# Batch 1's projections placed among the first maxima, and three operands' parts made by GpSimd

## The chip, the cores and the metric

One core of a Trainium2 chip runs the whole program in one launch. It has five instruction streams that meet only through semaphores: TensorE (PE) for matrix products, VectorE (DVE), ScalarE (ACT) and GpSimd (POOL) for the rest, and SyncE (SP), which issues most of the DMAs. Each engine takes its instructions strictly in the order in which they were written. The time is the device time of one execution in microseconds; the kernel before took 1213.18 us (median of 3 runs, 1212.56 to 1214.47).

## The reference

Four batches of 1024 tokens with 128 features go through three steps, each on the layer-normalised input and added to it: an expert-choice feed-forward (8 experts, each takes the 256 tokens of a batch with the highest affinity), attention with 16 heads of 8 features and rotary angles in three axes, and the same feed-forward again.

```python
x = x + 0.5 * ffn(layernorm(x))
x = x + attn(layernorm(x))
x = x + 0.5 * ffn(layernorm(x))

# ffn: affinity = softmax(x @ gate.T); per expert the 256 best tokens of a batch
h = silu(x_in @ w_gate.T) * (x_in @ w_up.T)
out[tokens of the expert] += gating * (h @ w_down.T)

# attn
q, k, v = x @ Wq + bq, x @ Wk + bk, x @ Wv + bv      # 16 heads of 8
q, k = rope3d(q), rope3d(k)                          # y * cos + rotated(y) * sin
out = softmax(q @ k.T / sqrt(8)) @ v @ Wo + bo
```

## The kernel before

**Passes.** The feed-forward runs as 16 passes (it = 0 to 15) before attention and 16 behind it; a pass is one expert on two batches. Batches 0 and 1 are done in passes 0 to 7, batches 2 and 3 in 8 to 15. A pass has four gate and up products (`gate_up`), the down product of the pass before (`down`), its outputs, and the choice and gathering of tokens for later passes. Its three weights come in two buffers each, loaded by `load_weights(j)` on SyncE; `gate_up(j, 0)` waits for all three. GpSimd issues the gathers of rows and the scatters that add the outputs to x in DRAM.

**Side work.** Between the products of a pass stand small steps at places (it, k), set by the table `place` in `tables()`. The keys ("s", m) are the preparation of attention for batches 0 and 1: m = 0 the rotated weights, 1 to 4 the transposes of the normalised x into ZT, and from 5 on five steps for each operand u. An operand u is q or k of batch u // 2 (u = 0 is q of batch 0, u = 3 is k of batch 1). Its five steps are four projections (w in two halves of 512 tokens, then the rotated weights wr in two halves) and one of values. In these steps VectorE adds the bias and multiplies by cos or sin (L1677), and adds the two products (L1692).

**Parts.** q and k are used in bfloat16 as sums of three parts, so each operand of 128 x 1024 goes through `high` (ScalarE rounds it, L934), `rest` (the operand less that part), `middle` (ScalarE rounds the rest, L938) and `lowest` (the rest less the middle part). For u = 0 and 1 VectorE does rest and lowest, for the others GpSimd (L673, L678). The parts stand in two buffers (u % 2) and go to DRAM (`store_parts`), from where `load(q)` fetches the rows of a group of heads. SyncE does all this in the order in which it is written, the weights among it.

**First maxima.** Attention has 16 groups, q = 0 to 15, four to a batch, so batch 1 is used from group 4 on. A group first needs the maximum of each row of scores: 32 pieces of two matmuls into one of two pA buffers (L1373), and a VectorE reduction for each (L1821). Behind pass 15 the 32 pieces of group 0 and 12 of group 1 run by themselves. Among them stands what is left of the preparation, in a table `window`: "T" are transposes for batches 2 and 3, "PR" the four projections of operands 4 to 7, into the three pS banks in rotation, with a value step into pO behind the fourth, and "m" the turn of the first maxima. Here ScalarE adds the bias (L1059), and GpSimd multiplies (`product`, L683) and adds (`add_products`, L688). VectorE computes the moments of batches 2 and 3 behind pieces 12 and 13 and their `scale_and_shift` behind 14 and 15; ScalarE takes the roots (`deviation`) and normalises (`normalise(6)`, `normalise(7)`).

**Groups.** Then group q runs its 64 score matmuls (L1458), 64 exponentials on ScalarE (L1115), 64 products with the values (L1437), and among them the pieces of the next groups. Behind 46 exponentials TensorE turns the next group's maxima (L1381), which GpSimd has cut in parts (`maxima`, L693 to L699), and ScalarE copies them as mT (L1124). In groups 0 and 1 ScalarE also has `middle(5)`, `high(6)`, `high(7)`, `middle(6)` and `middle(7)` between its exponentials.

Of the kernel before, what the change touches and what calls it, by code (L numbers as in the profile page):

```python
# [12 lines left out]
B, N, D = 4, 1024, 128  # L13
# [3 lines left out]
P = 128  # L17
CH = N // P
T = B * CH
# [10 lines left out]
NF = 11 + ROUNDS  # L30
# [13 lines left out]
def tables():  # L44
# [6 lines left out]
    for m in range(5, 25):  # L51
        place[divmod(55 + m, 5)] = ("s", m)
# [32 lines left out]
    for u, at in ((4, 22), (5, 28), (6, 32), (7, 37)):  # L85
        for i in range(4):
            window[divmod(at + i, 32)] = ("PR", u, i)
# [4 lines left out]
def program(nc, t, x1, out, zd, qk, vp, md, ud, dd, rd):  # L92
    ctx = ExitStack()
    with ctx:
# [6 lines left out]
        def sem(name):  # L101
# [114 lines left out]
        pairs = {4: (scr[:, 0, :], scr[:, 2, :]), 5: (scr[:, 1, :], scr[:, 3, :]), 6: (room[:, 0, :], room[:, 1, :]),  # L216
                 7: (U[1][:, :], U[2][:, :])}
# [161 lines left out]
        def _(sp):  # L379
# [55 lines left out]
            def store_values(b):  # L435
                if b < 2:
                    sp.wait_ge(*was_read(("s", 10 * b + 14)))
                else:
                    sp.wait_ge(s_vs, 2 * b - 2)
# [104 lines left out]
            store_values(1)  # L544
            load_weights(16)
            load_weights(17)
            for b in range(2, B):
                sp.wait_ge(s_scat[b], 256)
                load_x(b, x1_in)
            store_parts(2)  # L550
# [51 lines left out]
        def _(pool):  # L602
# [76 lines left out]

            def product(u, i):  # L680
# [4 lines left out]
            def add_products(u):  # L685
                a, b = pairs[u]
                pool.wait_ge(s_mul, 2 * (u - 3))
# [117 lines left out]
            scatter(RUN - 1)  # L805
            rest(2)
            rest(3)
            lowest(2)
# [21 lines left out]
            product(7, 1)  # L830
            lowest(5)
            add_products(7)
            rest(6)
# [7 lines left out]
            for q in range(1, NQ):  # L841
                if q in (7, 11, 15):
                    context(q // 4 - 1)
                maxima(q)
                if q == 1:
                    lowest(6)
                    rest(7)
                    lowest(7)
# [38 lines left out]
        def _(act):  # L887
# [152 lines left out]
            middle(2)  # L1040
            middle(3)

# [19 lines left out]
            def value_rows(u):  # L1062
                act.wait_ge(s_v, u - 3)
                values_out(u, pO[:, :]).then_inc(s_vs, 1)

            deviation(6)
            deviation(7)
            act.wait_ge(s_sd, 8)
            S.activation(warm[:, :], sd[:, 0:8], ACT.Exp)
            normalise(6)  # L1070
            turned_half(0)
            turned_half(1)
            normalise(7)
# [28 lines left out]
            def result(q, half):  # L1102
                k = q % 3
                act.wait_ge(s_pv, 16 * q + 8 * half + 12)
                act.wait_ge(s_ust[k], 128 * (q // 3) + 16)
                S.activation(U[k][:, half * 512:(half + 1) * 512], pO[:, :], ACT.Copy).then_inc(s_U, 1)  # L1106

            def group(q):
                k = q % 3
                for s in range(16):  # L1110
# [840 lines left out]
```

## Time and profile before

| | us |
|---|---|
| median of 3 runs | 1213.18 |
| profiled execution, its own time | 1224.46 |
| its span, first to last instruction | 1222.7 |
| TensorE busy in it | 1085.8 (89%) |
| VectorE busy | 981.3 (80%) |
| ScalarE busy | 774.1 (63%) |
| GpSimd busy | 580.7 (47%) |

The profile is one execution, recorded by the hardware. Passes 0 to 15 take the first 308 us of it, the first maxima 308 to 372, the 16 groups 372 to about 960, and the second feed-forward the rest. A row of a timeline gives start, length, engine, line, operation, result and source, how many were merged, and in brackets how long the engine had been idle before and what ended that. A number such as L1373 is a line of the kernel. The lengths of neighbours overlap by some tenths of a microsecond, since a record ends when the last result is written. "PEclk", the clock column, is the granted share of 2.4 GHz: 1.00, or 0.50 for 1.2 GHz.

### The profile page before, as it was taken

What the parts mean: (1) busy time and instruction counts of PE and PEld (TensorE: products, weight loads), DVE (VectorE), ACT (ScalarE), POOL (GpSimd) and SP (SyncE); (2) the same over time, 40 slices, a digit from 0 to 9 for tenths busy, and PEclk for the clock granted to TensorE, in tenths of its full rate; (3) what the DMA queues carried; (4) which work ended last, traced back from release to release, by engine and by line L of the source; (5) the groups of instructions that cost most, each with busy time, mean ns of one, the idle gap of its engine ahead of it and who ended that gap; (6) DMA issues with size and microseconds to landing.
All of it is one profiled execution on the core that took longest, in us unless ns stands there. A gap on an engine that the chain in (4) does not pass through costs nothing. (4 is left out here: it accounts for less than half of the span.)

```text
span 1222.7 us, 25195 instructions
## 1 busy us (share of the span) xinstructions
PE 1085.8 (89%) x9412; PEld 471.6 (39%) x9412; DVE 981.3 (80%) x1938; ACT 774.1 (63%) x1466; POOL 580.7 (47%) x610
## 2 busy tenths in 40 slices
PE   6189899899499899999999999999999889899994
PEld 6056566566132122222222222222222247566663
DVE  5755966565979899999999999999997576876641
ACT  3044232532258899999989999899999936222220
POOL 4035878665456331000011476355621077677886
PEclk6589999999688899999999999999999999999997
DMA  9014456448703131211021111211220126345553
GB/s 268 27 44 115 89 100 142 93 79 185 192 36 96 33 90 43 58 43 47 21 58 42 42 51 40 53 42 41 64 68 11 24 66 151 82 90 102 113 101 29
DMA packets 93072, 93.84 MB, mean 77 GB/s; under 512 B 14684, under 2 KB 70236, under 8 KB 92920
## 3 DMA queue, kind: packets, MB, share of 16 engines
q1 hardware_dynamic: 70424, 75.46, 22.2%
q0 software_dynamic: 22528, 16.79, 10.4%
q8 instruction: 74, 1.21, 0.4%
q14 instruction: 46, 0.38, 0.1%
HBM read 64.02 MB, written 30.13 MB: 77 GB/s over the span
## 5 line engine op out<-in xcount | busy, mean ns | idle before, releaser
L1821 DVE TENSOR_REDUCE mx<-pA 128x2 f32<-128x1024 f32 x512 | 585.9, 1217 | 20.1 <-PE pA L1373 19.4
L1115 ACT ACTIVATE Pt<-pS 128x512 f32<-128x512 f32 x1024 | 556.3, 596 | 34.5 <-PE pS L1458 29.0
L1437 PE MATMUL pO<-Pt,Vst 128*16 128x256 f32 x4096 | 322.7, 387 | 13.4 <-ACT U L1106 12.8
L1012 ACT ACTIVATE Pt<-pS 128x512 f32<-128x512 f32 x128 | 76.3, 596 | 206.9 <-PE pS L1287 177.4
L622 POOL DMA_INDIRECT xg<-zd,idx x128 | 125.9, 983 | 165.0 <-DVE idx L1628 95.1
L1373 PE MATMUL pA<-Kst,Qst 48*128 48x512 bf16 x704 | 140.8, 397 | 20.1 <-DVE mx L1821 18.4
L1287 PE MATMUL pS<-Pt,wg 128*128 128x512 f32 x256 | 139.8, 629 | 13.4 <-issue 7.5
L1437 PEld LDWEIGHTS pO<-Pt,Vst 128*16 128x16 f32 x4096 | 68.2, 94 | 207.0 <-issue 109.1
L1458 PE MATMUL pS<-Qst,Kst 51*128 51x512 bf16 x704 | 139.2, 391 | 7.5 <-ACT Pt L1115 4.6
L693 POOL TENSOR_TENSOR mparts<-mx,onesm 128x32 bf16<-128x32 f32 x16 | 4.0, 252 | 262.4 <-DVE mx L1826 206.2
L1298 PEld LDWEIGHTS pA<-wd,Pt 128*128 128x128 f32 x960 | 113.5, 192 | 17.0 <-issue 17.0
L1613 DVE TENSOR_SCALAR onehot<-slots,slotT 128x256 bf16<-128x256 bf16 x512 | 119.1, 312 | 0.4
L645 POOL DMA_INDIRECT x<-Pt,idx x64 | 102.3, 1598 | 32.0 <-issue 17.4
L1298 PE MATMUL pA<-wd,Pt 128*128 128x128 f32 x960 | 114.2, 275 | 0.0
L1458 PEld LDWEIGHTS pS<-Qst,Kst 51*128 51x128 bf16 x704 | 34.4, 92 | 157.3 <-ACT Pt L1115 144.3
L1655 DVE TENSOR_TENSOR Pt<-Pt,pS 128x512 f32<-128x512 f32 x64 | 43.9, 686 | 37.0 <-PE pS L1288 16.8
L1288 PE MATMUL pS<-Pt,wu 128*128 128x512 f32 x128 | 68.7, 619 | 0.0
L1288 PE MATMUL pO<-Pt,wu 128*128 128x512 f32 x128 | 66.3, 600 | 0.0
L1655 DVE TENSOR_TENSOR Pt<-Pt,pO 128x512 f32<-128x512 f32 x64 | 43.8, 685 | 27.3 <-PE pO L1288 18.8
L1458 PE MATMUL pS<-pair 51*128 51x512 bf16 x320 | 62.4, 386 | 1.1 <-ACT Pt L1115 0.4
L1373 PE MATMUL pA<-pair 48*128 48x512 bf16 x320 | 61.9, 383 | 0.6 <-DVE mx L1821 0.6
L1003 ACT ACTIVATE Pt<-pA 128x512 f32<-128x512 f32 x32 | 19.1, 597 | 67.5 <-remote 48.6
(224 smaller groups left out, 1181.7 us busy)
## 6 DMA issues: line engine op xcount, KB each, us to landing
wg<-w_gate_dram SPq DMA_DIRECT2D x32, 256.0 KB
wu<-w_up_dram SPq DMA_DIRECT2D x32, 256.0 KB
wd<-w_down_dram SPq DMA_DIRECT2D x32, 256.0 KB
qk<-parts SPq DMA_DIRECT2D x64, 96.0 KB
Kst<-qk SPq DMA_DIRECT2D x132, 32.0 KB
zd<-Z SPq DMA_DIRECT2D x8, 512.0 KB
vp<-pair SPq DMA_DIRECT2D x4, 1024.0 KB, 4.6
Vst<-vp SPq DMA_DIRECT2D x16, 256.0 KB
```

Source lines behind the costliest of these rows:

```text
L622: pool.indirect_dma_start(xg[p][:, k, :], None, zd[j // E % 2], bass.IndirectOffsetOnAxis(idx[j % 6][:, k:k + 1], 0)).then_inc(s_gath[p], 16)
L645: pool.indirect_dma_start(acc, bass.IndirectOffsetOnAxis(rows[j % 6][:, k:k + 1], 0), ye[j % 2][:, k, :], None, compute_op=ALU.add).then_i ...
L1115: S.activation(Pt[:, s % 4, j, r * 512:(r + 1) * 512], pS[:, bank_of(k, 4 * s + 2 * j + r), :], ACT.Exp, scale=SCALE).then_inc(s_exp, 1)
L1287: M.matmul(pG[u % 2], wg[p][:, u * P:(u + 1) * P], xt[:, p, :], start=True, stop=True).then_inc(s_gate, 1)
L1288: M.matmul(pU[u % 2], wu[p][:, u * P:(u + 1) * P], xt[:, p, :], start=True, stop=True).then_inc(s_up, 1)
L1298: last = M.matmul(pY[:, k * D:(k + 1) * D], hid[p][:, i, k * P:(k + 1) * P], wd[p][:, i, :], start=(i == 0), stop=(i == IC - 1))
L1373: last = M.matmul(pA[ring[q, a] % 2][:, r, :], Qst[k][64 * r:64 * r + 48, j, c * P:(c + 1) * P], Kst[k][64 * r:64 * r + 48, j, half * 512: ...
L1437: last = M.matmul(pO[32 * h:32 * h + 16, cols], Vst[k][:, s % 8, h, :], Pt[:, s % 4, h // 2, (h % 2) * 512 + 256 * a:(h % 2) * 512 + 256 * ...
L1458: last = M.matmul(pS[:, bank_of(k, n + r), :], Kst[k][64 * r:64 * r + ROWS, j, (s % 8) * P:(s % 8 + 1) * P], Qst[k][64 * r:64 * r + ROWS, ...
L1613: last = V.tensor_scalar(onehot[:, b, c, :], slots[:, :], slotT[j // E % 2][:, c * HB + b, e:e + 1], None, ALU.is_equal)
L1655: V.tensor_tensor(hid[it % 2][:, u, :], sg[:, u % 2, :], pU[u % 2], ALU.mult).then_inc(s_hid, 1)
L1821: V.reduce_max(mx2[:, k, 2 * j:2 * j + 2, c, half], pA[ring[q, a] % 2][:, :, :], AX.X).then_inc(s_Ar, 1)
```

## The change

Operands 2 and 3 (batch 1) leave passes 14 and 15 and become "PR" entries of the window, at pieces 0, 2, 4, 6 and 8, 10, 12, 13. With that ScalarE adds their bias and GpSimd multiplies and adds, where VectorE did both. The steps `high(2)`, `middle(2)`, `high(3)` and `middle(3)` of ScalarE move in between its work for the normalisations, and the value store of batch 1 moves behind the loads of x on SyncE. The high and middle parts of operands 6 and 7 and the middle part of 5 are made by GpSimd with a product with ones (`own_part`), and GpSimd's second maxima stand ahead of operand 7's sum instead of behind it. The last down product no longer waits for step ("s", 24).

```diff
-    for m in range(5, 25):
+    for m in range(5, 15):
         place[divmod(55 + m, 5)] = ("s", m)
...
-    for u, at in ((4, 22), (5, 28), (6, 32), (7, 37)):
-        for i in range(4):
-            window[divmod(at + i, 32)] = ("PR", u, i)
+    for u, ats in ((2, (0, 2, 4, 6)), (3, (8, 10, 12, 13)), (4, range(22, 26)), (5, range(28, 32)), (6, range(32, 36)), (7, range(37, 41))):
+        for i, at in enumerate(ats):
+            window[divmod(at, 32)] = ("PR", u, i)
...
             load(0)
             load(1)
-            store_values(1)
             load_weights(16)
             load_weights(17)
             for b in range(2, B):
                 sp.wait_ge(s_scat[b], 256)
                 load_x(b, x1_in)
+            store_values(1)
             store_parts(2)
...
+            def own_part(u, i, ready):
+                a = pairs[u][i]
+                pool.wait_ge(*ready)
+                if i == 0:
+                    pool.wait_ge(s_partst[u % 2], 128 * (u // 2))
+                GP.tensor_tensor(parts[:, u % 2, i, :].rearrange("p (a n) -> p a n", n=P), a.rearrange("p (a n) -> p a n", n=P),
+                                 ones[:, :].unsqueeze(1).to_broadcast([P, N // P, P]), ALU.mult).then_inc((s_hi, s_mid)[i], 1)
...
             scatter(RUN - 1)
+            product(2, 0)
+            product(2, 1)
+            add_products(2)
+            product(3, 0)
             rest(2)
+            product(3, 1)
+            add_products(3)
+            lowest(2)
             rest(3)
-            lowest(2)
             lowest(3)
...
             product(7, 1)
+            own_part(5, 1, (s_rest, 6))
             lowest(5)
+            own_part(6, 0, (s_roped, 7))
+            rest(6)
+            maxima(1)
+            own_part(6, 1, (s_rest, 7))
+            lowest(6)
             add_products(7)
-            rest(6)
+            own_part(7, 0, (s_roped, 8))
+            rest(7)
+            own_part(7, 1, (s_rest, 8))
+            lowest(7)
...
-                maxima(q)
-                if q == 1:
-                    lowest(6)
-                    rest(7)
-                    lowest(7)
+                if q > 1:
+                    maxima(q)
...
-            middle(2)
-            middle(3)
...
+            for u in (2, 3):
+                for i in range(4):
+                    projected(u, i)
+                value_rows(u)
+            high(2)
             deviation(6)
+            middle(2)
             deviation(7)
             act.wait_ge(s_sd, 8)
             S.activation(warm[:, :], sd[:, 0:8], ACT.Exp)
             normalise(6)
+            high(3)
             turned_half(0)
             turned_half(1)
+            middle(3)
             normalise(7)
...
-                    if q == 0 and s == 8:
-                        middle(5)
-                    if q == 0 and s == 9:
-                        high(6)
-                    if q == 0 and s == 13:
-                        high(7)
-                    if q == 0 and s == 15:
-                        middle(6)
-                    if q == 1 and s == 2:
-                        middle(7)
...
-                pe.wait_ge(*was_read(("s", 24) if j < RUN else ("f", 3, NF - 1)))
+                pe.wait_ge(*was_read(("s", 14) if j < RUN else ("f", 3, NF - 1)))
```

TensorE, pass 15 and the start of the first maxima. L1287 and L1288 are gate and up, L1298 and L1313 down, L1206 a projection, L1212 a value step, L1373 a piece. Before:

```order
L1206 MATMUL pA<-ZT,wq 128x512
L1298 MATMUL pA<-wd,Pt 128x128 x8
L1206 MATMUL pA<-ZT,wr 128x512
L1287 MATMUL pS<-Pt,wg 128x512
L1288 MATMUL pS<-Pt,wu 128x512
L1206 MATMUL pA<-ZT,wr 128x512
L1287 MATMUL pS<-Pt,wg 128x512
L1288 MATMUL pO<-Pt,wu 128x512
L1212 MATMUL pA<-wv,ZT 128x128 x4
L1313 MATMUL pA<-wd,Pt 128x128 x16
L1373 MATMUL pA<-Kst,Qst 128x512 x42
```

and now (L1306, L1307, L1317, L1332, L1225, L1231 and L1392 are the same functions):

```order
L1317 MATMUL pA<-wd,Pt 128x128 x16
L1306 MATMUL pS<-Pt,wg 128x512
L1307 MATMUL pS<-Pt,wu 128x512
L1306 MATMUL pS<-Pt,wg 128x512
L1307 MATMUL pO<-Pt,wu 128x512
L1332 MATMUL pA<-wd,Pt 128x128 x16
L1392 MATMUL pA<-Kst,Qst 128x512 x2
L1225 MATMUL pS<-ZT,wq 128x512
L1392 MATMUL pA<-Kst,Qst 128x512 x4
L1225 MATMUL pS<-ZT,wq 128x512
L1392 MATMUL pA<-Kst,Qst 128x512 x4
L1225 MATMUL pS<-ZT,wr 128x512
```

The five steps have left the pass, and projections stand between the pieces from the first on.

GpSimd, from the last scatters (L645) to the product of operand 4. Before:

```order
L645 DMA x<-Pt,idx 2048x128 x16
L673 TENSOR_TENSOR scr<-scr,parts 128x1024 x2
L678 TENSOR_TENSOR parts<-scr,parts 128x1024 x2
L683 TENSOR_TENSOR scr<-scr,cos 128x1024
L683 TENSOR_TENSOR scr<-scr,sin 128x1024
L688 TENSOR_TENSOR scr<-scr 128x1024
```

and now (L693 is `product`, L698 `add_products`, L674 `rest`, L679 `lowest`):

```order
L646 DMA x<-Pt,idx 2048x128 x16
L693 TENSOR_TENSOR scr<-scr,cos 128x1024
L693 TENSOR_TENSOR scr<-scr,sin 128x1024
L698 TENSOR_TENSOR scr<-scr 128x1024
L693 TENSOR_TENSOR scr<-scr,cos 128x1024
L674 TENSOR_TENSOR scr<-scr,parts 128x1024
L693 TENSOR_TENSOR scr<-scr,sin 128x1024
L698 TENSOR_TENSOR scr<-scr 128x1024
L679 TENSOR_TENSOR parts<-scr,parts 128x1024
L674 TENSOR_TENSOR scr<-scr,parts 128x1024
L679 TENSOR_TENSOR parts<-scr,parts 128x1024
L693 TENSOR_TENSOR scr<-scr,cos 128x1024
```

Six operations have come in ahead of operand 4, and the parts of 2 and 3 are made between them.

GpSimd in groups 0 and 1, from the last products of operand 7 (U) on, with the second maxima (mparts). Before:

```order
L683 TENSOR_TENSOR U<-U,sin 128x1024
L678 TENSOR_TENSOR parts<-scr,parts 128x1024
L688 TENSOR_TENSOR U<-U 128x1024
L673 TENSOR_TENSOR onehot<-onehot,parts 128x1024
L693 TENSOR_TENSOR mparts<-mx,onesm 128x4x8
L695 TENSOR_TENSOR mres<-mx,mparts 128x32
L697 TENSOR_TENSOR mparts<-mres,onesm 128x4x8
L699 TENSOR_TENSOR mparts<-mres,mparts 128x4x8
L678 TENSOR_TENSOR parts<-onehot,parts 128x1024
L673 TENSOR_TENSOR U<-U,parts 128x1024
L678 TENSOR_TENSOR parts<-U,parts 128x1024
```

and now (L687 is `own_part`):

```order
L693 TENSOR_TENSOR U<-U,sin 128x1024
L687 TENSOR_TENSOR parts<-scr,ones 128x1024
L679 TENSOR_TENSOR parts<-scr,parts 128x1024
L687 TENSOR_TENSOR parts<-onehot,ones 128x1024
L674 TENSOR_TENSOR onehot<-onehot,parts 128x1024
L703 TENSOR_TENSOR mparts<-mx,onesm 128x4x8
L705 TENSOR_TENSOR mres<-mx,mparts 128x32
L707 TENSOR_TENSOR mparts<-mres,onesm 128x4x8
L709 TENSOR_TENSOR mparts<-mres,mparts 128x4x8
L687 TENSOR_TENSOR parts<-onehot,ones 128x1024
L679 TENSOR_TENSOR parts<-onehot,parts 128x1024
L698 TENSOR_TENSOR U<-U 128x1024
```

Products with ones have come in, two of them ahead of the maxima (five in all, the last two behind the sum of operand 7), and that sum stands behind the maxima.

## Rows read from the trace of the kernel before

**Rows 1.** Busy time by stage; columns: stretch, its length, busy of each engine, clock, DMA
```profile
272.40:287.60 15.20, 15.20 (x70) 9.41 (x69) 9.91 (x16) 5.66 (x11) 11.02 (x7) 1.00 0.92 220
...
308.50:336.00 27.50, 11.11 (x40) 2.01 (x40) 26.82 (x58) 8.38 (x15) 14.11 (x8) 0.56 0.73 177
...
372.40:411.00 38.60, 33.32 (x275) 6.76 (x273) 33.02 (x28) 30.26 (x55) 22.26 (x14) 0.78 0.38 97
...
447.40:484.00 36.60, 35.68 (x389) 8.56 (x385) 36.54 (x34) 35.62 (x69) 4.19 (x13) 1.00 0.17 36
```

**Rows 2.** Timeline of TensorE around passes 14 and 15; start, us, instruction, idle before
```profile
278.49 1.02 PE L1206 MATMUL pA<-ZT,wq 128*128 128x512 f32 x2
...
286.72 1.05 PE L1212 MATMUL pA<-wv,ZT 128*128 128x128 f32 x8
...
303.62 3.81 PE L1313 MATMUL pA<-wd,Pt 128*128 128x128 f32 x32 [1.08 <-ACT pair L926]
308.54 0.61 PE L1373 MATMUL pA<-Kst,Qst 48*128 48x512 bf16 x4 [1.11 <-DVE Pt L1646]
```

**Rows 3.** Timeline of SyncE's DMA issues behind pass 13
```profile
273.84 6.69 SPq L432 DMA_DIRECT2D qk<-parts  x8
...
281.62 0.49 SPq L395 DMA_DIRECT2D wd<-w_down_dram  x1
...
297.47 0.35 SPq L463 DMA_DIRECT2D Vst<-vp  x1
```

**Rows 4.** Busy time in two stretches of pass 14; last columns: DMA share, GB/s
```profile
273.40:277.10 3.70, 3.70 (x13) 1.79 (x12) 2.25 (x3) 2.01 (x3) 3.09 (x3) 1.00 0.84 292
...
281.00:285.50 4.50, 4.50 (x17) 2.30 (x16) 3.81 (x8) 1.19 (x2) 2.28 (x1) 1.00 1.05 255
```

**Rows 5.** Timeline of TensorE, a projection at either clock
```profile
342.57 2.08 PE L1206 MATMUL pS<-ZT,wq 128*128 128x512 f32 x2
...
352.42 1.13 PE L1206 MATMUL pS<-ZT,wq 128*128 128x512 f32 x2
```

**Rows 6.** Timeline of VectorE, first maxima and group 0
```profile
308.97 14.80 DVE L1821 TENSOR_REDUCE mx<-pA 128x2 f32<-128x1024 f32 x13 [0.94 <-PE pA L1373]
...
331.03 0.17 DVE L1528 SCALAR_TENSOR_TENSOR shift<-mv,rstd 128x8 f32<-128x8 f32 x1
...
399.40 2.12 DVE L1826 TENSOR_TENSOR mx<-mx 128x32 f32<-128x32 f32 x1
...
444.49 0.19 DVE L1826 TENSOR_TENSOR mx<-mx 128x32 f32<-128x32 f32 x1
```

**Rows 7.** Timeline of GpSimd, from the last scatter to group 0
```profile
314.75 1.56 POOL L645 DMA_INDIRECT x<-Pt,idx  x1 [0.30 <-issue]
...
345.45 2.34 POOL L683 TENSOR_TENSOR scr<-scr,cos 128x1024 f32<-128x1024 f32 x1 [20.77 <-ACT scr L1059]
...
381.57 2.35 POOL L683 TENSOR_TENSOR U<-U,cos 128x1024 f32<-128x1024 f32 x1
...
399.12 2.36 POOL L688 TENSOR_TENSOR U<-U 128x1024 f32<-128x1024 f32 x1
```

**Rows 8.** Timeline of ScalarE, groups 0 to 2
```profile
373.08 1.10 ACT L1115 ACTIVATE Pt<-pS 128x512 f32<-128x512 f32 x2
...
383.98 12.03 ACT L1115 ACTIVATE Pt<-pS 128x512 f32<-128x512 f32 x22 [0.68 <-PE pS L1458]
395.89 1.06 ACT L938 ACTIVATE parts<-scr 128x1024 bf16<-128x1024 f32 x1
...
405.24 0.27 ACT L1124 ACTIVATE mT<-pS 96x128 bf16<-96x128 bf16 x1 [1.64 <-PE pS L1381]
...
447.35 0.28 ACT L1124 ACTIVATE mT<-pS 96x128 bf16<-96x128 bf16 x1
...
483.98 0.27 ACT L1124 ACTIVATE mT<-pS 96x128 bf16<-96x128 bf16 x1
```

**Rows 9.** Timeline of TensorE, group 0
```profile
404.89 0.31 PE L1381 MATMUL pS<-identb,mparts 128*96 128x128 bf16 x1 [2.42 <-POOL mparts L699]
```

More of the change, by code:

```diff
@@ L215, in program @@
         room = onehot[:, :, :, :].rearrange("p b c s -> p (b c s)").bitcast(F32).rearrange("p (i n) -> p i n", i=2)
-        pairs = {4: (scr[:, 0, :], scr[:, 2, :]), 5: (scr[:, 1, :], scr[:, 3, :]), 6: (room[:, 0, :], room[:, 1, :]),
-                 7: (U[1][:, :], U[2][:, :])}
+        pairs = {u: (scr[:, u % 2, :], scr[:, 2 + u % 2, :]) for u in range(2, 6)}
+        pairs |= {6: (room[:, 0, :], room[:, 1, :]),
+                  7: (U[1][:, :], U[2][:, :])}
         dens = sb("dens", [P, P], F32)
@@ L435, in store_values @@
             def store_values(b):
-                if b < 2:
-                    sp.wait_ge(*was_read(("s", 10 * b + 14)))
+                if b == 0:
+                    sp.wait_ge(*was_read(("s", 14)))
                 else:
-                    sp.wait_ge(s_vs, 2 * b - 2)
+                    sp.wait_ge(s_vs, 2 * b)
                 sp.dma_start(vp[b * G:(b + 1) * G].rearrange("g p f -> p g f"),
@@ L686, in add_products @@
                 a, b = pairs[u]
-                pool.wait_ge(s_mul, 2 * (u - 3))
+                pool.wait_ge(s_mul, 2 * (u - 1))
                 GP.tensor_tensor(a, a, b, ALU.add).then_inc(s_roped, 1)
@@ L1062, in value_rows @@
             def value_rows(u):
-                act.wait_ge(s_v, u - 3)
+                act.wait_ge(s_v, u - 1)
                 values_out(u, pO[:, :]).then_inc(s_vs, 1)
+            for u in (2, 3):
[3 more added lines that the diff above has]
+            high(2)
             deviation(6)
+            middle(2)
             deviation(7)
@@ L1105, in result @@
                 act.wait_ge(s_ust[k], 128 * (q // 3) + 16)
+                if (q, half) == (1, 0):
+                    act.wait_ge(s_parts, 2 * B)
                 S.activation(U[k][:, half * 512:(half + 1) * 512], pO[:, :], ACT.Copy).then_inc(s_U, 1)
@@ L1397, in window_use @@
                     if i == 0:
-                        pe.wait_ge(s_winr, win["T", 2 * (b - 2) + 1] + 1)
-                    last = project(op, (wq, wr)[i // 2], 2 * (b - 2) + i % 2, bank)
+                        pe.wait_ge(*(was_read(("s", 4)) if b == 1 else (s_winr, win["T", 2 * (b - 2) + 1] + 1)))
+                    last = project(op, (wq, wr)[i // 2], 2 * (b % 2) + i % 2, bank)
                 else:
@@ L1405, in window_use @@
                     u = key[1]
-                    if u > 4:
-                        pe.wait_ge(s_vs, u - 4)
+                    if u > 2:
+                        pe.wait_ge(s_vs, u - 2)
                     project_values(u, pO[:, :]).then_inc(s_v, 1)
@@ L1414, in _ @@
             pe.wait_ge(s_ye, RUN)
-            pe.wait_ge(*was_read(("s", 24)))
+            pe.wait_ge(*was_read(("s", 14)))
             pe.nop().then_inc(s_mt, 1)
@@ L1425, in _ @@
             pe.wait_ge(s_winr, len(win))
-            pe.wait_ge(s_vs, 4)
+            pe.wait_ge(s_vs, 6)
             pe.nop().then_inc(s_pv, 4)
```

## Prediction

> **What bounds the kernel now.** I read the busy time by stage first [rows 1]. In passes 14 and 15 TensorE is full (15.20 us of 15.20). In the first maxima (308.5 to 336.0) VectorE is full (26.82 of 27.5) and TensorE idles at half its clock. In the first two attention groups (372.4 to 411.0) nobody is full and the mean clock is 0.78; from 447.4 on VectorE is at 36.54 of 36.60. So the three stages that the change touches have three limits, and each of its parts is priced in its own. What is won there carries to the end: the groups behind run at a fixed pace (next paragraph), and nothing they load is late.
>
> The pace of a group is read from ScalarE's copy mT, once a group [rows 8]: 447.35 to 483.98 is 36.63 us, the steady value. 405.24 to 447.35 is 42.11, so 5.5 us are lost there. From the group's first exponential (373.08) to 405.24 are 32.2 us, where a steady group takes 46 exponentials at 0.545 (22 of them in 12.03), one result copy before and one after (1.1): 26.2. Lost: 6.0. Together 11.5 us.
>
> Durations are of the profiled execution: span 1222.7, its own time 1224.5, 11 us above the median 1213.18 that I predict from; I take the difference over unscaled (scaling by 0.99 changes it by 0.1).
>
> **Passes 14 and 15 (term A).** Each loses 4 projections and 4 value matmuls on TensorE. A projection shows 1.02 us [rows 2], two back to back start 0.86 apart as the records overlap, a value step 0.89 from 1.05: 4 x 0.86 + 0.89 = 4.33 us a pass, all on the path, since TensorE is full. In pass 15 also the 1.08 us go in which the last down product waited for ScalarE's value copy [rows 2]. If TensorE stays the limit: 2 x 4.33 + 1.08 = 9.7 us.
>
> What is late next in pass 14 is its successor's weights. SyncE issues pass 15's weights behind eight part stores (273.84, 6.69 us) and ends at 281.62 + 0.49 = 282.1 [rows 3]. Nothing in that chain moves: it hangs on batch 0's values, which stay in pass 13. The DMA engines are full, share 1.05 from 281.0 to 285.5. Up to 277.1 they move 292 GB/s x 3.7 us = 1.08 MB, which is the value store [rows 4]. Behind it come 0.77 MB of parts, 0.77 of weights and a scatter (0.3 with what it reads), 1.85 MB at pass 14's 220 GB/s [rows 1]: 8.4 us, weights in at 285.5. TensorE would want them at 287.61 - 4.33 = 283.3; today it comes at 287.6 and never notices. So pass 14 gives 1.9, not 4.3 (ends: 0 if they land at 287.6, 4.3 if at 283.3). Waiting 2.4 us may also drop the clock: TensorE's 2.42 us wait at 404.9 was followed by 5.5 us at 1.2 GHz [rows 9]. Half a chance of 1 us: 0.5.
>
> Then the first maxima's operands. store_parts(1) comes 2 us earlier, its landing at most 1 (full DMA engines), so load(0), whose last issue is 297.47 [rows 3], ends near 297 and lands near 299.5. TensorE arrives at 285.5 + (308.54 - 287.61) - 4.33 - 1.08 = 301.0: no new wait. Term A: -1.9 - 5.4 + 0.5 = -6.8; ends -9.0 (held by load(0)) and -3.9.
>
> **First maxima, 44 pieces (term B).** S is the first piece (308.54 now). VectorE takes 13 pieces in 14.80 us, 1.13 each [rows 6]. Added: 8 projections and 2 value steps on TensorE among pieces 0 to 13. At 2.4 GHz a projection is 1.13 with 1.06 between starts, at 1.2 GHz 2.08 and 2.0 [rows 5]; a piece takes 0.33 or 0.6 on TensorE. Fast: 14 x 0.33 + 8 x 1.06 + 2 x 0.95 = 15.0 against VectorE's 15.8: hidden, save 0.5 where a value step bunches. Slow throughout: 28.2, of which some 5 lie beside batch 2's moments on VectorE: +7.6. Today the clock falls 3.4 us into this stage because TensorE idles, which it would no longer do; I take the fast end, +0.7.
>
> On GpSimd six operations of 2.35 come in (14.1 us) before batch 2's first product, today at 345.45 after 20.77 us idle [rows 7]: 6.7 us of room, part of which goes in waits for high and middle, and ScalarE's two high and two middle copies stand between its normalisations. I follow the chain: the last scatter ends at S + 7.8 as now (it hangs on the last outputs), products and sum of operand 2 at S + 15, first product of 3 at 17.3, high(2) 18.3, rest 20.5, sum of 3 at 25.2, high(3) 26.2 to 27.4, rest(3) 29.6, lowest(3) 34.5. Batch 2's product starts at S + 36.9 now. Fits by 2.4. high(3) stands ahead of the ZT copies at S + 29.3: fits. middle(3) delays normalise(7) by 1.0, of which 0.5 arrives.
>
> VectorE itself is touched. Its 128x32 maximum takes 0.19 us in the other groups, but 2.12 at 399.40, exactly while GpSimd's sum runs from 399.12 for 2.36 [rows 6, 7]: a two-operand VectorE instruction waits for a GpSimd instruction that reads. Today GpSimd is idle from 324.7 to 345.4, over all of batch 2's and 3's moments; now it computes there. Exposed are veps twice and shift twice (0.17 each [rows 6]), each against a 2.1 to 2.35 us operation: nothing to 9.4 us, a mean of 1.2 where GpSimd is busy. By the times above veps(6) falls in a gap, the other three hit for 1.8, 0.8 and 0.7: +3.0. Pieces before 20 set the end, so this is on the path; it hides the 0.5 of middle(3). The Trainium skill has this rule ("SBUF — State Buffer", Who interferes with whom): a VectorE instruction with two SBUF inputs, or in a two-port mode, and a reading GpSimd instruction block each other whole, while a reduction never takes part. The reductions agree: 1.13 each, though GpSimd computes beside the last seven of the 13. Without the rule term B would be 3 us smaller.
>
> Term B: +0.7 + 3.0 = +3.7; ends 0 and +12. SyncE: store_values(1) only moves behind two X loads; batch 1 is first loaded at group 2.
>
> **First two groups (term C).** The 11.5 lost consist of: five ScalarE copies of 0.95 (395.89 is one [rows 8]), 4.75; a 1.2 GHz stretch at the start, 14 exponentials from 373.08 to 383.98 instead of in 7.6, 3.3; the wait of TensorE for GpSimd's maxima (2.42 [rows 9]) and the slow stretch behind it, the rest, 3.5. The five copies go to GpSimd at about 2.35. Maxima 1 stand seven operations behind 381.57 [rows 7]: 15.7, at 397.3, with VectorE's maximum not before 399: no wait, and no collision as GpSimd waits then. The other part stores follow by 416, needed at group 4. The 3.3 stay, since nothing before them on TensorE changes, and the pace cannot beat VectorE's 36.63: 0.4 more. Term C: -(11.5 - 3.3 - 0.4) = -7.8; ends -3.5 (only the wait goes) and -11.
>
> **Sum.** -6.8 + 3.7 - 7.8 = -10.9. I forecast 1202.5 us.
>
> **Rivals.**
> R1, weights bind pass 15 fully and the added projections meet the slow clock: -3.9 + 7.5 + 3.0 - 7.8 is about -1 at the extreme; the middle of it -5: 1208. For: the full DMA engines, the half clock in this stage. Against: TensorE would be busy there.
> R2, GpSimd's port costs nothing and the clock stays up: -9.0 + 0.7 - 7.8 = -16: 1197. Against: the 2.12 row.
> R3, the copies moved off ScalarE buy little because VectorE, next at 36.54 of 36.60, is the limit, and the slow stretch spreads: term C -3.5, total -6.6: 1206.5. Against: VectorE idles whenever those copies run (33.0 of 38.6).
> R4, slower: the in-order chain GpSimd-ScalarE for batch 1. high(3) stands ahead of the ZT copies and needs GpSimd's eighth step. The chain has 3 us of room at high(3); each us by which the first product comes later than S + 12 delays group 0 by one. At S + 27 it eats the 14.6 of A and C; at S + 30 the time is 3 slower, 1216. It needs the last scatters to land 20 us late; they end at 316.3 now [rows 7], though into full DMA engines.
> R5, no net effect: B near +11, within 0.2% (2.4 us, about what a measurement of this kernel can tell from no change).
>
> **Chances.** Forecast (1199 to 1206) 0.55, R2 0.12, R1 0.13, R3 0.10, R4 0.04, R5 0.06. Range 1196 to 1209. Faster by over 0.2% 0.90, within 0.06, slower 0.04.
>
> **What would show it.** A: gate_up of pass 15 starts near 285.5 after an idle, first piece near 301.5; wrong if the idle is missing (then -9) or the piece is after 304.5. B: 1.1 us projections between pieces, first group 66 to 68 us after the first piece (63.9 now), VectorE's small instructions of 1 to 2.4 us; wrong if they stay at 0.17. C: mT at 36.7 instead of 42.1 between groups 0 and 1, no TensorE wait on GpSimd there. The forecast is wrong if batch 1's parts are what batch 2's ZT copies wait for.

## The result and the profile after

The changed kernel took 1207.53 us (median of 5 runs, 1204.31 to 1210.77), the kernel before 1213.52 beside it: ratio 0.9946, 95% interval 0.9929 to 0.9964, that is 6.5 us less (4.4 to 8.6). The recorded ratio isn't the quotient of the medians; these are 6.0 apart. A second session gave 1207.03 against 1213.60, ratio 0.9945 (0.9927 to 0.9963). I had forecast 10.9 less. The sign and the three parts are right; the terms A and B have a wrong size, and 1207.53 lies outside the band of 1199 to 1206 that I gave my own account, though inside the whole range. Two executions far longer than all others, 1512.09 us of the kernel before and 2499.92 of before_gate, are left out of all ratios.

Spans can't be subtracted here. Pass 14 starts at 272.41 in the trace before and at 265.15 in the one after, though nothing ahead of it differs; over all profiled executions of this study it starts anywhere from 260.3 to 274.2. From there to the end the two take 950.3 and 943.8, which are 6.5 apart as the times are. So every trace below is read from pass 14's start, in three stretches that answer to the three terms: to the first piece (A), from there to the first exponential of group 0 (B), and from there to the second copy mT that follows, 447.35 in [rows 8] (C).

| us | A | B | C | A+B+C |
|---|---|---|---|---|
| before | 36.13 | 64.54 | 74.27 | 174.94 |
| after | 32.51 | 71.13 | 64.50 | 168.14 |
| difference | -3.6 | +6.6 | -9.8 | -6.8 |
| forecast | -6.8 | +3.7 | -7.8 | -10.9 |
| after, second session | 32.87 | 67.92 | 64.35 | 165.14 |

The busy time by stage of the changed kernel, columns as in [rows 1]:

```profile
265.10:279.30 14.20, 11.09 (x54) 6.86 (x53) 6.21 (x11) 5.66 (x11) 10.61 (x8) 0.97 0.90 231
279.30:297.70 18.40, 17.25 (x82) 11.42 (x82) 5.00 (x12) 2.39 (x4) 7.71 (x6) 0.84 0.68 151
297.70:325.00 27.30, 16.43 (x66) 6.00 (x66) 26.09 (x52) 12.33 (x24) 23.33 (x13) 0.90 0.57 156
368.80:406.70 37.90, 36.61 (x351) 8.27 (x351) 36.90 (x35) 34.88 (x67) 35.85 (x20) 0.91 0.37 92
433.30:469.90 36.60, 35.67 (x389) 8.57 (x385) 36.54 (x34) 35.64 (x68) 4.27 (x13) 1.00 0.14 36
```

Pass 14 is no longer full (11.09 us of 14.20). The first maxima now run at a clock of 0.90 instead of 0.56, with VectorE still the full engine and GpSimd at 23.33 instead of 14.11. The groups behind are what they were.

**A.** The first matmuls of passes 14 and 15 in the kernel before:

```profile
272.41 1.02 PE L1287 MATMUL pS<-Pt,wg 128*128 128x512 f32 x2
...
287.61 1.02 PE L1287 MATMUL pS<-Pt,wg 128*128 128x512 f32 x2
```

The changed kernel at the same places and up to the first piece:

```profile
265.15 1.02 PE L1306 MATMUL pS<-Pt,wg 128*128 128x512 f32 x2
...
275.17 1.02 PE L1307 MATMUL pO<-Pt,wu 128*128 128x512 f32 x2
279.34 2.05 PE L1306 MATMUL pS<-Pt,wg 128*128 128x512 f32 x2 [3.15 <-issue]
281.18 1.91 PE L1307 MATMUL pS<-Pt,wu 128*128 128x512 f32 x2
282.88 1.91 PE L1306 MATMUL pS<-Pt,wg 128*128 128x512 f32 x2
284.59 1.39 PE L1307 MATMUL pO<-Pt,wu 128*128 128x512 f32 x2
285.81 3.73 PE L1317 MATMUL pA<-wd,Pt 128*128 128x128 f32 x32
...
297.66 0.39 PE L1392 MATMUL pA<-Kst,Qst 48*128 48x512 bf16 x2 [1.11 <-DVE Pt L1665]
```

Pass 15 starts 14.19 us after pass 14 instead of 15.20, behind an idle of 3.15 us. This row names nothing that ended the idle; that it was the weights is shown below, by issuing them earlier. And its four gate and up steps, 3.44 us at 2.4 GHz (4 x 0.86), take 6.47 (279.34 to 285.81): they run at 1.2 GHz, all but the end of the last.

SyncE over the same time, for [rows 3]:

```profile
266.58 7.13 SPq L433 DMA_DIRECT2D qk<-parts  x8
...
274.76 0.46 SPq L396 DMA_DIRECT2D wd<-w_down_dram  x1
275.27 5.05 SPq L433 DMA_DIRECT2D qk<-parts  x8
282.86 2.14 SPq L462 DMA_DIRECT2D Qst<-qk  x6
```

**B.** VectorE's small instructions, 0.17 us each before [rows 6]. veps is the variance plus epsilon, shift the mean times the reciprocal of the deviation, each for batch 2 and then for batch 3:

```profile
315.99 2.10 DVE L1542 TENSOR_SCALAR veps<-mv 128x8 f32<-128x8 f32 x1
...
321.48 1.00 DVE L1542 TENSOR_SCALAR veps<-mv 128x8 f32<-128x8 f32 x1
...
323.74 1.14 DVE L1547 SCALAR_TENSOR_TENSOR shift<-mv,rstd 128x8 f32<-128x8 f32 x1
...
326.16 0.80 DVE L1547 SCALAR_TENSOR_TENSOR shift<-mv,rstd 128x8 f32<-128x8 f32 x1
```

Together 5.04 instead of 0.68. GpSimd beside them now runs one instruction right behind the other, where it was idle for 20.77 us before [rows 7]:

```profile
315.72 2.34 POOL L693 TENSOR_TENSOR scr<-scr,cos 128x1024 f32<-128x1024 f32 x1
318.02 2.12 POOL L674 TENSOR_TENSOR scr<-scr,parts 128x1024 f32<-128x1024 f32 x1
...
339.82 2.35 POOL L693 TENSOR_TENSOR scr<-scr,cos 128x1024 f32<-128x1024 f32 x1 [2.39 <-ACT scr L1078]
```

The first veps starts 0.27 us behind a product of 2.34 and ends with it. The last row is batch 2's first product: GpSimd still waits 2.39 us for ScalarE before it, so R4's chain is not what sets the end. Batch 2's first projection on TensorE is the mark by which B is split further down:

```profile
334.43 2.04 PE L1225 MATMUL pS<-ZT,wq 128*128 128x512 f32 x2 [0.23 <-ACT ZT L1068]
```

**C.** ScalarE in the first groups, for [rows 8], and GpSimd's second maxima:

```profile
368.79 2.19 ACT L1144 ACTIVATE Pt<-pS 128x512 f32<-128x512 f32 x4
...
377.64 15.32 ACT L1144 ACTIVATE Pt<-pS 128x512 f32<-128x512 f32 x28 [0.87 <-PE pS L1477]
...
396.65 0.27 ACT L1153 ACTIVATE mT<-pS 96x128 bf16<-96x128 bf16 x1
...
433.29 0.27 ACT L1153 ACTIVATE mT<-pS 96x128 bf16<-96x128 bf16 x1
```
```profile
394.10 0.25 POOL L703 TENSOR_TENSOR mparts<-mx,onesm 128x32 bf16<-128x32 f32 x1 [0.96 <-DVE mx L1845]
```

28 exponentials run in a row where one of the part copies came after 22, and the two copies mT are 36.64 us apart, the steady pace, where they were 42.11. It is GpSimd that waits for VectorE now (0.96 us), not TensorE for GpSimd (2.42 [rows 9]).

### The profile page after: what moved, and what is told of

It reads as the page before. It is cut to its first block and busy times, and to the rows that moved or that the text cites. A ratio compares the mean times of both kernels' runs of the same rounds, so it can differ in the third digit from the quotient of the medians.

```text
span 1208.9 us, 25202 instructions
## 1 busy us (share of the span) xinstructions
PE 1084.2 (90%) x9412; PEld 474.2 (39%) x9412; DVE 976.4 (81%) x1928; ACT 775.5 (64%) x1469; POOL 606.4 (50%) x621
## 3 DMA queue, kind: packets, MB, share of 16 engines
q8 instruction: 74, 1.21, 0.4%
## 5 line engine op out<-in xcount | busy, mean ns | idle before, releaser
L1392 PE MATMUL pA<-Kst,Qst 48*128 48x512 bf16 x704 | 137.8, 388 | 18.5 <-DVE mx L1840 17.4
L1306 PE MATMUL pS<-Pt,wg 128*128 128x512 f32 x256 | 140.7, 632 | 7.7 <-issue 4.9
L1317 PEld LDWEIGHTS pA<-wd,Pt 128*128 128x128 f32 x960 | 114.0, 193 | 16.9 <-issue 16.1
L1317 PE MATMUL pA<-wd,Pt 128*128 128x128 f32 x960 | 114.5, 276 | 0.0
L1307 PE MATMUL pS<-Pt,wu 128*128 128x512 f32 x128 | 68.4, 617 | 0.0
L1307 PE MATMUL pO<-Pt,wu 128*128 128x512 f32 x128 | 67.5, 610 | 0.0
L1392 PE MATMUL pA<-pair 48*128 48x512 bf16 x320 | 61.2, 378 | 0.6 <-DVE mx L1840 0.6
```

Of the source, the lines that this page charges most:

```text
L1306: M.matmul(pG[u % 2], wg[p][:, u * P:(u + 1) * P], xt[:, p, :], start=True, stop=True).then_inc(s_gate, 1)
L1307: M.matmul(pU[u % 2], wu[p][:, u * P:(u + 1) * P], xt[:, p, :], start=True, stop=True).then_inc(s_up, 1)
L1317: last = M.matmul(pY[:, k * D:(k + 1) * D], hid[p][:, i, k * P:(k + 1) * P], wd[p][:, i, :], start=(i == 0), stop=(i == IC - 1))
L1392: last = M.matmul(pA[ring[q, a] % 2][:, r, :], Qst[k][64 * r:64 * r + 48, j, c * P:(c + 1) * P], Kst[k][64 * r:64 * r + 48, j, half * 512: ...
```

## The experiments

Eleven kernels (one of them the changed kernel again), in three sessions: the first four of the table behind "before", the next four, and the last three. Each was timed beside the kernel before, whose median was 1222.68, 1213.60 and 1226.12 in them, so only ratios carry over. The table gives the ratio with its interval, what it makes of the session's time before, and the stretches of the one profiled execution. Single executions differ by some us outside the three stretches too; the stretches show the mechanism, the ratio the size, and where the two disagree the text says so.

| kernel | ratio (95%) | us | A | B | C | sum |
|---|---|---|---|---|---|---|
| before | | | 36.13 | 64.54 | 74.27 | 174.94 |
| parts_only | 0.9941 (0.9919-0.9964) | -7.2 | 36.16 | 64.77 | 65.56 | 166.49 |
| proj_only | 0.9973 (0.9950-0.9995) | -3.3 | 32.03 | 68.86 | 74.27 | 175.16 |
| weights_first | 0.9943 (0.9922-0.9963) | -7.0 | 29.65 | 69.23 | 64.80 | 163.68 |
| kept_warm | 0.9964 (0.9950-0.9979) | -4.4 | 32.44 | 69.05 | 65.52 | 167.01 |
| after_again | 0.9945 (0.9927-0.9963) | -6.7 | 32.87 | 67.92 | 64.35 | 165.14 |
| gate_first | 0.9888 (0.9864-0.9912) | -13.6 | 27.87 | 69.15 | 65.59 | 162.61 |
| kept_warm_short | 0.9919 (0.9893-0.9946) | -9.8 | 29.95 | 68.14 | 64.91 | 163.00 |
| reductions | 0.9931 (0.9909-0.9952) | -8.4 | 31.66 | 65.47 | 65.48 | 162.61 |
| before_gate | 1.0000 (0.9987-1.0013) | 0.0 | 36.13 | 63.39 | 73.29 | 172.81 |
| gate_eps | 0.9894 (0.9874-0.9914) | -13.0 | 28.36 | 67.01 | 65.02 | 160.39 |
| warm_turn | 0.9857 (0.9822-0.9892) | -17.5 | 27.14 | 63.27 | 65.65 | 156.06 |

**The parts alone.**
```
 kernel before, and in GpSimd's program:
+            own_part(5, 1, (s_rest, 6))
             lowest(5)
+            own_part(6, 0, (s_roped, 7)); rest(6); maxima(1); own_part(6, 1, (s_rest, 7)); lowest(6)
             add_products(7)
+            own_part(7, 0, (s_roped, 8)); rest(7); own_part(7, 1, (s_rest, 8)); lowest(7)
-                    (ScalarE's middle(5), high(6), high(7), middle(6), middle(7) in groups 0 and 1)
```


> The kernel before with the parts' half of the change alone (operand 5's second part and operands 6 and 7's parts made by GpSimd, second maxima ahead of them); batch 1's projections stay in passes 14 and 15. Theory 1 (the stages add up, as the changed kernel's trace has them: first exponential to second copy mT 64.5 us where the kernel before has 74.3): 9.8 us less than before, 1203.7 us; nothing else in the trace moves. The prediction's term C, -7.8, would be 1205.7. Rival R3 (VectorE is the limit once ScalarE is relieved, only TensorE's wait for the second maxima goes): -3.5, 1210. If the gain needs the later start of the changed kernel's attention (parts stores that would otherwise collide), it is also under 5.

7.2 us less (4.4 to 9.9; the medians are 6.3 apart); A and B as before to 0.3 us, C 65.56 instead of 74.27, 8.7 less. R3's 3.5 lies outside the interval of the ratio. The gain doesn't need the other half.

**Batch 1's projections alone.**
```
 changed kernel, and in GpSimd's and ScalarE's programs the lines above back as in the kernel before
```


> The changed kernel with the parts' half undone: only batch 1's projections are moved among the first maxima. Theory 1 (stages add): the changed kernel's trace has -3.6 in passes 14 and 15 and +6.6 from the first piece to the first exponential, so this kernel is 3.0 us slower than the kernel before, 1216.5. The prediction's terms A and B, -6.8 and +3.7, would make it 3.1 faster, 1210.4. Rival: the move pays only together with the other half or not at all, within 1 us of before. In the trace: first piece 32.5 us after pass 14's start as in the changed kernel, first exponential 71 us behind it.

C is 74.27 to the digit, A is 4.1 less and B 4.3 more: in the trace the move gives nothing (+0.2). Its 12 runs lie between 1213.33 and 1224.66, four of them up to 1217.53 and eight from 1220.36 on, and the profiled one is the slowest. The ratio says 3.3 less (0.6 to 6.1), the medians are only 0.7 apart. So the +3.0 that I had read out of the first trace after was too dark, and the forecast's -3.1 is inside the interval, but between nothing and 6 us the experiment doesn't decide. The ratios of the two halves add up to -10.5 where the changed kernel has -6.5 and -6.7, which their intervals allow; the stretches add up to -8.2 against -6.8 and -9.8.

**All of pass 15's weights ahead of batch 0's value store**, gate and up ahead of its part stores too.
```
-            store_values(0)
+            sp.wait_ge(s_up, 56);    wg, wu of pass 15
             store_parts(0)
-            load_weights(15)
+            sp.wait_ge(s_down, 14);  wd of pass 15
+            store_values(0)
             store_parts(1)
```


> The changed kernel with pass 15's three weight transfers issued ahead of batch 0's part stores and value store (wg and wu after their buffers are free, wd next). Theory 1 (TensorE's 3.15 us idle before pass 15's first gate and up product is the landing of the weights, and the 1.2 GHz stretch behind it, 279.34 to 285.81 instead of 3.44 us, is the price of that idle): both go, first piece 26.5 to 28 us after pass 14's start instead of 32.5, up to 6 us faster than the changed kernel, unless the first maxima's X operand or the batch-0 parts now land late: then 2 to 4. Rival (idle ends by something else, the weights have landed): 0, same idle. Second rival (the full DMA engines only pass the delay on): the idle is gone but TensorE waits the same time before the first piece, 0.

As the lines above show, only gate and up stand ahead of the part stores; the down weights stand behind the first eight of them.

The idle and the half clock behind it are gone, pass 15 starts 10.88 us after pass 14 and its four steps take 3.44: the idle was the wait for the weights. But the first piece gains only 2.9 of 6.3 us, as it now waits itself:

```profile
300.35 0.53 PE L1396 MATMUL pA<-Kst,Qst 48*128 48x512 bf16 x2 [4.60 <-DMA Vst<-vp]
300.81 2.07 PE L1229 MATMUL pS<-ZT,wq 128*128 128x512 f32 x2
```

The operand load behind batch 0's stores is the next wait, and the clock falls in front of the first projection. The time (-7.0) doesn't differ from the changed kernel's (-6.5 and -6.7 in the other sessions).

**TensorE kept busy through the wait, too long and right.**
```
 at the end of pass 14:
+                    pe.wait_ge(s_ye, 14)
+                    for n in range(28):      # kept_warm_short: 12
+                        M.matmul(pY[:, 0:P], ones[:, :], ones[:, :], start=True, stop=True)
```


> The changed kernel with 28 matmuls of 128x128 on constants, into a bank that is rewritten, put on TensorE at the end of pass 14, where it otherwise waits 3.15 us for pass 15's weights. They are extra work and no part of the result. Theory 1 (the half clock behind the wait costs 3.0 us of its own): the idle is filled, the clock stays at 2.4 GHz into pass 15, 2.5 to 3.0 us faster than the changed kernel though it does more work. Rival (the slow gate and up products wait for weights that arrive in pieces, or the clock falls for another reason): 0, or up to 0.5 slower for the added work.

> The changed kernel with 12 instead of 28 matmuls on constants at the end of pass 14. 28 took 6.42 us, past the landing of the weights, so that run lost 2.9 us and gained the 3.0 of the half clock: nothing in the sum. 12 take 2.75, within the 3.15 us wait. Theory 1 (the half clock is the price of TensorE's wait): pass 15 starts 14.2 us after pass 14 and runs at full clock, first piece 29.5 us after pass 14's start, 3.0 faster than the changed kernel. Rival (the clock needs more than this little work): the stretch at 1.2 GHz stays, 0.

With 28 the added work lasts 6.42 us and pass 15 starts 2.9 us later than in the changed kernel, yet the first piece comes at 32.44 (32.51 there): the half clock is gone and pays for it. The 2.5 to 3.0 us that I expected to gain didn't come, since the added work outlasts the wait. With 12, TensorE's timeline reads:

```profile
274.04 2.84 PE L1361 MATMUL pA<-ones 128*128 128x128 f32 x24
277.71 1.10 PE L1306 MATMUL pS<-Pt,wg 128*128 128x512 f32 x2 [0.83 <-issue]
278.64 1.02 PE L1307 MATMUL pS<-Pt,wu 128*128 128x512 f32 x2
```

The weights land no sooner (14.56 us after pass 14's start, 14.83 in the changed kernel beside it), but the steps behind run at full clock: first piece at 29.95 instead of 32.87, and 9.8 us under the kernel before where the changed kernel is 6.7. Behind pass 15's start the changed kernel takes 18.04 us beside it and 18.32 in its first run, this one 15.39: the half clock is worth 2.6 to 2.9 us in the trace, which is shown by adding work. In time the gain over the changed kernel is likely, but the two intervals overlap.

**The changed kernel again**, as the yardstick of that session.

> The changed kernel itself, unaltered, as the yardstick for the others on the same chip. Its first profiled execution had 103.6 us from pass 14's start to the first exponential, the three kernels with batch 1 moved that were run since had 98.9 to 101.5. If 71.1 us from the first piece to the first exponential was partly luck (VectorE's small instructions met GpSimd for 4.4 us, and the clock rose 1.3 us later than elsewhere), this run has 69 to 70; if it belongs to the kernel, 71 again. Time against the kernel before: -4 to -9 us by the first runs.

B is 67.92, and the whole difference to 71.13 lies behind batch 2's first projection (36.82 us behind the first piece here, 36.77 there): here the clock rises 2 us after it, there 9 us. So 1.6 either way of B is no property of the kernel. veps and shift took 5.07 us together here too.

**Gate and up weights first, value store ahead of the down weights.**
```
-            store_values(0)
+            sp.wait_ge(s_up, 56);    wg, wu of pass 15
             store_parts(0)
-            load_weights(15)
+            store_values(0)
+            sp.wait_ge(s_down, 14);  wd of pass 15
             store_parts(1)
```


> The changed kernel with pass 15's gate and up weights ahead of batch 0's part stores, then the parts, the value store, and the down weights last. In the run with all three weights first the 3.15 us idle and the half clock behind it were gone, but TensorE waited 4.60 us before the first piece, for an operand load that starts once batch 0's parts and values have landed (19.0 us after pass 14's start against 17.7 in the changed kernel); its value store was issued at 7.6 us. Theory 1: with the value store at about 5 us the load starts near 17.7 again, TensorE waits 3 us there, first piece 28.3 us after pass 14's start (32.5 in the changed kernel, 29.65 with all three first): 4.2 faster than the changed kernel. Rival (the DMA engines are full, bytes decide and not their order): 29.6, the wait only stays where it was. Second rival (the down weights come too late now): an idle appears before pass 15's first down product.

```profile
272.66 1.10 PE L1310 MATMUL pS<-Pt,wg 128*128 128x512 f32 x2 [1.34 <-issue]
...
288.15 0.39 PE L1396 MATMUL pA<-Kst,Qst 48*128 48x512 bf16 x2 [1.24 <-DMA Vst<-vp]
```

Two waits of 1.3 us in place of one of 3.15 and one of 4.60, neither followed by a slow stretch, and none before the down product. First piece at 27.87 (expected 28.3), and the time is 13.6 us under the kernel before: 6.9 better than the changed kernel in the same session, with intervals apart. It was the order of the issues, not the bytes.

The traces of that session show only part of the 6.9. A is 5.0 shorter than in the changed kernel, B and C are 1.2 longer each, and from pass 14's start to the end the two take 937.5 and 940.4. The other 4.4 us of the profiled pair lie ahead of pass 14, where the kernels are the same: between 200 and 240 us the mean clock is 1.00 in this execution and 0.91 to 0.92 in the other. Whether that goes with the kernel or with the execution no run decides. So the 5.0 of A are shown to be the order's, the rest of the 6.9 is not.

**The same order in the kernel before.**
```
 kernel before, with the five lines of gate_first
```


> The kernel before with one edit: pass 15's gate and up weights issued ahead of batch 0's part stores, the value store behind those, the down weights last. The same order made the changed kernel 7.0 us faster by the medians (-6.6 against -13.6 to the kernel before). Theory 1 (that gain is only the wait which the change opened): here TensorE has its four projections and a value step in either pass and the weights land before it asks for them, so nothing moves, within 1 us of the kernel before; pass 14 to pass 15 15.2 us, first piece 36.1 behind pass 14's start. Rival (the old order costs the kernel before too, through full DMA engines): 2 to 5 us faster.

Ratio 1.0000 within 0.13%; A is 36.13 as before. The order is worth something only once the projections are gone from pass 14: what it repairs is the wait that the change opened.

**Reductions in place of the four small instructions.** This kernel leaves out epsilon and the product with the reciprocal, so it measures the four instructions and can't replace them.
```
+                if i in (6, 7):
+                    V.reduce_max(veps[:, tiles(i)], mv[:, tiles(i), 1:2], AX.X).then_inc(s_ve, 1)
+                    return
 (shift likewise from mv[:, tiles(i), 0:1])
```


> The changed kernel with veps and shift of batches 2 and 3 computed by VectorE reductions of one input: epsilon and the product with the deviation's reciprocal are left out of them. Theory 1 (a VectorE instruction of that kind waits for a GpSimd instruction that reads, a reduction does not): all four take 0.2 us instead of 2.10, 1.00, 1.14 and 0.80, and the first exponential comes 3.4 to 4.4 us earlier after the first piece than in the changed kernel, near 66 to 66.7 (64.5 in the kernel before). Rival (they are slow because of what they are or where they stand, not because of GpSimd, or the first maxima are bound elsewhere): durations as before or the time given back before ZT, 0 to 1.

```profile
313.37 0.16 DVE L1543 TENSOR_REDUCE veps<-mv 128x8 f32<-128x8 f32 x1
...
316.92 0.16 DVE L1543 TENSOR_REDUCE veps<-mv 128x8 f32<-128x8 f32 x1
...
318.36 0.16 DVE L1551 TENSOR_REDUCE shift<-mv 128x8 f32<-128x8 f32 x1
...
319.79 0.16 DVE L1551 TENSOR_REDUCE shift<-mv 128x8 f32<-128x8 f32 x1
```
```profile
327.42 2.05 PE L1225 MATMUL pS<-ZT,wq 128*128 128x512 f32 x2 [0.24 <-ACT ZT L1068]
```

Same place, same size, GpSimd computing beside them: 0.16 each. Batch 2's first projection comes 32.38 us after the first piece instead of 36.77, so the 4.4 us were on the path to that mark, to the last tenth. By the medians 1.7 of it reaches the end, but the intervals overlap. The Trainium skill ("SBUF — State Buffer", Who interferes with whom) has exactly this split, reductions free and an instruction with two SBUF inputs or in a two-port mode locked out; the runs agree, 0.16 against 0.80 to 2.10.

**Epsilon by ScalarE, and TensorE kept busy in the first maxima.** Two versions on top of gate_first, with the full result.
```
 gate_eps:
+                    S.activation(sd[:, tiles(i)], mv[:, tiles(i), 1], ACT.Sqrt, bias=eps[:, :]).then_inc(s_sd, 1)
                     (for i in (6, 7), and VectorE's veps instruction is gone for them)
 warm_turn, behind pieces 14 to 19 besides:
+            DUMMIES = {14: 5, 15: 10, 16: 6, 17: 4, 18: 3, 19: 3}
+                    pe.wait_ge(s_vs, 2)
+                    for n in range(DUMMIES[a]):
+                        M.matmul(pO[:, 0:P], ones[:, :], ones[:, :], start=True, stop=True)
```


> The changed kernel with pass 15's gate and up weights first, and epsilon of batches 2 and 3 added by ScalarE as the bias of its square root instead of by a VectorE instruction. That instruction took 0.41 and 1.74 us in the run with the gate weights first (2.10 and 1.00 in the changed kernel) where it takes 0.17 beside an idle GpSimd. Port theory: 1.8 us fewer from the first piece to the first projection of batch 2 (35.83 there), 34.0; but the two shifts, earlier now, may meet GpSimd's next operation for longer than 1.15 and 0.80: then 34 to 35.8. Rival (the rest of the chain decides): 35.8 again. The epsilon by bias adds nothing on ScalarE.

> The kernel with gate weights first and epsilon as a bias, and 31 matmuls of 128x128 on constants behind pieces 14 to 19, where TensorE otherwise waits for VectorE's moments and shifts (4.74, 1.82 and 1.47 us idle). Extra work, no part of the result. Theory (the half clock under batch 2's first four projections, 2.07 us each instead of 1.13, is the price of those waits, and sits on the path): full clock there, four projections and their pieces in 5.5 instead of 8.1 us, so 2.5 to 3.3 us fewer from batch 2's first projection to the first exponential, and 3 us off the time. Rival: the added matmuls delay pieces as much as they save, 0 or slower; or the clock falls all the same and they cost 1 to 3 us.

gate_eps has batch 2's first projection at 34.58 us behind the first piece instead of 35.83 in gate_first. It waited 2.08 us before its first piece, and one of the projections behind took 2.07 us, so its moments began 16.81 us behind the first piece instead of 15.98; from there on the gain is 2.1. But its ratio is gate_first's: inconclusive in time. In warm_turn the projections that took 2.07 take 1.10 to 1.13:

```profile
332.69 1.10 PE L1234 MATMUL pS<-ZT,wq 128*128 128x512 f32 x2 [0.23 <-ACT ZT L1077]
...
334.04 1.13 PE L1234 MATMUL pS<-ZT,wq 128*128 128x512 f32 x2
```

B is 63.27, below the kernel before, although 31 matmuls were added: 3.7 less than in gate_eps (67.01), of which 1.8 behind batch 2's first projection (30.62 instead of 32.43) and 1.9 ahead of it, where pieces too ran at half clock. Of the 1.9, 0.8 is gate_eps's slow projection, ahead of the added matmuls (15.98 us to the moments here), so they are worth 2.9 in this pair of executions, within the 2.5 to 3.3 expected. 17.5 us under the kernel before (13 to 22; the medians are 16.7 apart) is the best kernel of the study. That it beats gate_eps itself (-13.0) is likely, but their intervals overlap.

## Why the prediction was right, and where its sizes were wrong

**The mechanism of A was right, its price was not.** The idle before pass 15 was forecast at 2.4 us and is 3.15, so pass 14 gives 1.0 and not 1.9. The step that failed is the clock: "Half a chance of 1 us: 0.5". It costs 2.8 to 3.0 in the two executions of the changed kernel, and kept_warm_short shows that it goes away when the wait is filled. I had a row that bore on it, a wait of 2.42 us [rows 9] that was followed by 5.5 us at 1.2 GHz. The error was in the pricing: where TensorE is the limit a us at half clock costs half a us, so 5.5 of them cost 2.7 and not 1; the 6.47 us of gate and up work here cost 3.0. And the chance of one half was too low, as each of the four waits over 3 us before pass 15 had its slow stretch. Pass 15's own saving of 5.4 is there: from its first down product on (285.81) to the first piece are 11.85 us, and 36.13 - 15.20 - 3.44 = 17.49 before, 5.6 less. So A is -3.6 for -6.8: 0.9 from the later weights, 2.5 from the clock, less 0.2. That is outside the ends that I gave A (-9.0 and -3.9), and by my own sign A is wrong: the first piece, counted from pass 14 before, comes at 272.41 + 32.51 = 304.9, after the 304.5 that I had set. The issue times on SyncE were as forecast to 0.4 us; the landing, 14.2 us after pass 14's start for 13.1, was not, and why the transfers took longer stays open.

**B: the port was right and its price too small.** +4.4 for +3.0; I had veps(6) fall in a gap, and it was hit hardest (2.10). Where the hits fall changes with GpSimd's phase: the first veps took 2.10 and 2.13 us in the changed kernel and 0.17, 0.17, 0.41, 1.10 and 1.21 in five of its variants, while the four together took 4.4 more than before in the first two and 3.4 to 3.5 more in all five. A schedule followed to the tenth of a us said 3.0 and the mean over the exposure, four times 1.2, says 4.8: the measured ones lie between, and neither would have told which instruction is hit. The 13 pieces with projections between them gave +0.8 (15.56 against 14.80; 0.7 forecast), and the clock stayed up there, as taken. Of the rest, 1.4, all but 0.1 lies behind batch 2's first projection, in the later rise of the clock there, which the second session doesn't show. So B's 71.13 is in part bad luck of the first execution: 67.92 in the second is within the 66 to 68 that I had named, and of B's miss of 2.9 about half is the port's and half this. (The 63.9 that I set beside them ends at 372.4, ahead of the first exponential, where this count has 64.54.) R4's chain held its room.

**C was too careful.** -9.8 and -9.9 in the changed kernel, -8.7 with the parts alone, for -7.8. Wait and copies are gone as forecast. What "the 3.3 stay" priced did not all stay: the slow exponentials at the start of group 0 end at 377.64, 8.9 us after the first, and not after 10.9 as in [rows 8]; and the 0.4 for the pace didn't come. In all executions with the parts' half the second copy mT follows the first by 36.63 or 36.64 us; what differs between them, 64.35 to 65.66, lies in group 0 and its slow stretch. R3 is out.

**Altogether** A took 3.2 from the forecast and B 2.9, C gave 2.0 back: -10.9 became -6.8. The two misses are in the stretches that batch 1's move touches; alone it is worth about what I forecast by the ratio (-3.3), and next to nothing by its medians and its trace, and this stays open. None of the rivals is the case: R1's half clock came, but after the wait in pass 15 and not under the added projections. The number alone would have spoken for R1 (1208) or R3 (1206.5) more than for mine (1202.5, where 1213.18 less 10.9 is 1202.3); it is the stretches that speak against them. And that C's surplus offset part of the two misses is luck.

## What to carry over

Work taken from a full engine uncovers whatever was hidden behind it. Ask what arrives next, and if it is a transfer, reorder its issue in the same change: this was worth 5 us of A here (6.9 by the times), and nothing at all in the kernel before. Price a wait of TensorE with the slow stretch behind it, in full where TensorE is the limit; a few matmuls on constants in the wait are the cheap test, and a cheap cure as long as they end before the wait does. When GpSimd is given work in a stretch where it was idle, look at every small VectorE instruction there, and ask whether ScalarE can take those on the path, as it took epsilon here.

## What I had not expected of the hardware

- TensorE's waits of 3.15, 3.56, 3.79 and 3.94 us before pass 15 (four executions of three kernels) and of 4.60 before the first piece were each followed by work at 1.2 GHz, those of 0.74 to 1.34 at these two places by none, and one of 2.08 before the first piece by a single projection of 2.07 us. But how much of it is slow differs: behind 3.15 all four gate and up steps, behind 3.56 the first took 1.10 and only the next two 1.86 and 1.91. So pass 15's four steps lost 3.0 us in one execution and 1.8 in another. Nor does a slow stretch end at a fixed distance from the work: behind batch 2's first projection it lasted 2 us in one execution and 9 in another of the same kernel.
- In the changed kernel the 13 pieces with eight projections among them held the clock at 2.4 GHz until TensorE next waited 3.71 us for VectorE, where the same pieces without them had lost it after 3.4 us (clock 1.00 from 308.5 to 311.9, 0.50 from there to 325.0).
- Kernels that are identical up to pass 14 reach it anywhere from 260.3 to 274.2 us. A difference of two spans means nothing here before it is split by a mark in the trace.
